# SyncE's queue walked head by head: weights loaded once per head, one output-weight buffer

## What is computed

```python
qkvz = (x @ W_qkvz).reshape(B, S, NK, 2 * DK + 2 * R * DV)     # 16 heads, R = 2
q, k, v, z = split(qkvz)
q, k, v = silu(conv4(q)), silu(conv4(k)), silu(conv4(v))
core = chunk_gated_delta_rule(l2norm(q), l2norm(k), v, g, beta)
x1 = core * silu(z)
x1 = x1 * rsqrt(mean(x1 * x1, -1) + EPS) * norm_weight
x = layernorm(x + x1.reshape(B, S, VD) @ W_out)
x = layernorm(x + ffn(x))                                       # ternary W_up, W_gate, W_down
```

## Time and profile before

| | |
|---|---|
| median of 3 executions | 4410.59 us |
| the profiled execution | 4409.74 us |
| its span, first to last instruction | 4408.0 us |
| granted TensorE clock, mean | 0.992 |
| PE busy | 4208.9 us, 95% |
| ACT busy | 3843.0 us, 87% |
| DVE busy | 3727.2 us, 85% |
| POOL busy | 2342.4 us, 53% |
| bytes moved on SP's queue | 575.59 MB, 40.6% of 16 DMA engines |

### The profile page before, as it was taken

One profiled execution on the slowest core, in us unless ns is written; L12 is line 12 of the kernel. 1 busy time (PEld: TensorE's weight loads), 2 busy tenths in 40 slices (PEclk: granted clock), 3 DMA queues, 4 the chain that ended last, 5 costly groups with the idle time before them and its releaser, 6 DMA issues. The chain is left out here.

```text
span 4408.0 us, 140088 instructions
## 1 busy us (share of the span) xinstructions
PE 4208.9 (95%) x44246; PEld 3698.7 (84%) x44246; DVE 3727.2 (85%) x6642; ACT 3843.0 (87%) x10855; POOL 2342.4 (53%) x3319
## 2 busy tenths in 40 slices
PE   3799999999999999999999999999999999999888
PEld 2688888888888888888888888888888888888745
DVE  5688888888888888888888888888888888888766
ACT  2699999999999999999999999999999999999755
POOL 3355555555555555555555555555555555555455
PEclk9999999999999999999999999999999999999999
DMA  5544444444444444444444434344444343434201
GB/s 182 180 131 146 130 145 133 142 134 141 134 140 135 140 135 140 139 136 139 136 142 132 145 130 146 129 143 132 147 128 150 125 153 122 153 123 154 72 6 34
DMA packets 450786, 584.82 MB, mean 133 GB/s; under 512 B 237472, under 2 KB 315552, under 8 KB 433184
## 3 DMA queue, kind: packets, MB, share of 16 engines
q1 hardware_dynamic: 449568, 575.59, 40.6%
q10 hardware_dynamic: 1152, 8.39, 0.5%
HBM read 533.81 MB, written 50.07 MB: 132 GB/s over the span
## 5 line engine op out<-in xcount | busy, mean ns | idle before, releaser
L1014 DVE SCALAR_TENSOR_TENSOR conv<-ps,cws,conv 128x511 f32<-128x511 f32 (+2 forms) x1536 | 1085.6, 742 | 59.8 <-ACT conv L892 39.9
L698 PE MATMUL ps<-xb,wb 128*128 128x512 f32 x3072 | 842.9, 409 | 25.7 <-DMA wb<-w_scratch 21.6
L698 PEld LDWEIGHTS ps<-xb,wb 128*128 128x128 f32 x3072 | 542.0, 190 | 127.5 <-issue 27.8
L1057 DVE CAST_PREDICATED pl<-masks,ps 128x512 f16<-128x512 uint16 x768 | 546.9, 712 | 55.3 <-PE ps L760 32.7
L953 ACT ACTIVATE t<-ps 128x512 f16<-128x512 f32 x768 | 465.9, 607 | 118.3 <-PE ps L768 107.1
L1263 POOL TENSOR_TENSOR xo<-xo,zs 128x512 f32<-128x512 f32 x128 | 163.8, 1280 | 717.0 <-DVE xo L1108 717.0
L1263 POOL TENSOR_TENSOR xo<-xo,home 128x512 f32<-128x512 f32 x128 | 162.8, 1272 | 699.4 <-DVE xo L1108 699.4
L957 ACT ACTIVATE u<-ps 128x512 f16<-128x512 f32 x768 | 473.2, 616 | 43.6 <-PE ps L773 43.6
L858 PE MATMUL ps<-wo,xt 128*128 128x256 f32 x3072 | 427.4, 289 | 33.6 <-DVE xt L1114 32.8
L712 PE MATMUL ps<-wb,xb 128*128 128x256 f32 x3072 | 428.5, 289 | 0.0
L858 PEld LDWEIGHTS ps<-wo,xt 128*128 128x128 f32 x3072 | 382.9, 190 | 47.7 <-issue 42.0
(11 more groups left out here) (188 smaller groups left out, 11701.8 us busy)
## 6 DMA issues: line engine op xcount, KB each, us to landing
xb<-x_scratch SPq DMA_DIRECT2D x128, 1024.0 KB, 5.9
wb<-w_scratch SPq DMA_DIRECT2D x128, 1024.0 KB, 5.6
decays<-rows_scratch SPq DMA_DIRECT2D x128, 512.0 KB, 3.7
wb<-w_scratch SPq DMA_DIRECT2D x128, 512.0 KB, 4.3
wo<-wout_scratch SPq DMA_DIRECT2D x128, 512.0 KB, 6.3
rk<-rk_scratch SPq DMA_DIRECT2D x128, 256.0 KB, 4.2
w_scratch<-wsplit SPq DMA_DIRECT2D x128, 192.0 KB, 3.2
wpiece<-in_Wqkvz SPq DMA_DIRECT2D x128, 96.0 KB, 2.5
```

Source lines behind the costliest of these rows:

```text
L698: last = nc.tensor.matmul(proj_bank[c][:, :], wb[:, pw, k * WCOL + c * D:k * WCOL + (c + 1) * D], xb[p][:, px, k * S:(k + 1) * S], start=( ...
L1014: nc.vector.scalar_tensor_tensor(out=conv[c][:, back:S], in0=proj_bank[c][:, 0:S - back], scalar=cws[p][:, c * TAPS + 3 - back:c * TAPS + ...
L1057: nc.vector.copy_predicated(halves(pl[l], l, 0), mask[:, None, :, :].broadcast_to([128, NU, C // (4 << l), 2 << l]), packed(p_bank, l)).th ...
```

## The change

Only SP's walk changes. It now goes through eight steps (one head) per turn of its loop, so that the stage functions know at build time which of the head's eight items, `q`, they are called for. `load_w`, `load_wz` and `load_wout` return at once unless `q` is 0. The wait on `rk_in` in `load_w` is gone; a wait on `ws_out` (the pieces of the coming head are in HBM) is added to all three. `wo` becomes a single buffer, and its load waits for the last out product of the item just before. PE's waits count heads in place of items.

```diff
-        wo = [sb(f"wo{p}", [128, 2, R, H], f32r) for p in range(2)]
+        wo = sb("wo", [128, 2, R, H], f32r)
...
+        def steps_by_head(engine, **parts):
...
+            first, last = -(-(3 - NEAR) // B), (ITS - FAR) // B
+            for s in range(-FAR, first * B):
+                step(s, s % B)
+            with engine.Fori(first, last) as j:
+                for q in range(B):
+                    step(B * j + q, q)
+            for s in range(last * B, ITS - NEAR):
+                step(s, s % B)
...
-            def load_w(a, p, _):
+            def load_w(a, q, _):
+                if q:
+                    return
+                ws_out.wait(sp, a + B - 1 - LEAD, 32)
                 proj_mm.wait(sp, a - 1, 4)
-                rk_in.wait(sp, a - 1, 16)
...
-            def load_wz(a, p, _):
+            def load_wz(a, q, _):
+                if q:
+                    return
+                ws_out.wait(sp, a + B - 1 - LEAD, 32)
                 z_mm.wait(sp, a - 1, 2)
...
-            def load_wout(b, p, _):
-                out_mm.wait(sp, b - 2, 2)
+            def load_wout(b, q, _):
+                if q:
+                    return
+                out_mm.wait(sp, b - 1, 2)
+                ws_out.wait(sp, b + B - 1 - LEAD, 32)
...
-                    pe.wait_ge(w_in.sem, w_in.at(a, 16))
+                    pe.wait_ge(w_in.sem, w_in.at(a // B, 16))
...
-                    pe.wait_ge(wz_in.sem, wz_in.at(a, 16))
+                    pe.wait_ge(wz_in.sem, wz_in.at(a // B, 16))
...
-                    pe.wait_ge(wo_in[p].sem, wo_in[p].at(b // 2, 16))
+                    pe.wait_ge(wo_in.sem, wo_in.at(b // B, 16))
```

More of the change, by code:

```diff
@@ L498, in delta_rule @@
         small_ready, cw_ready = signal("small_ready"), signal("cw_ready")
-        wo_in = [signal(f"wo_in{p}", 16) for p in range(2)]
+        wo_in = signal("wo_in", 16)
         rows_in = signal("rows_in", 16)
@@ L598, in steps, with step @@
                 step(s, s % 2)
+        def steps_by_head(engine, **parts):
+            def step(s, q):
+                for offset, stage, *n in ORDER:
+                    if stage in parts and not (isinstance(s, int) and not 0 <= s + offset < ITS):
+                        parts[stage](s + offset, (q + offset) % B, *n)
+            first, last = -(-(3 - NEAR) // B), (ITS - FAR) // B
[6 more added lines that the diff above has]
+                step(s, s % B)
         @block.sync
@@ L605, in _, with load_x @@
             sp.wait_ge(made.sem, made.at(0, MADE))
-            def load_w(a, p, _):
+            def load_w(a, q, _):
+                if q:
+                    return
+                ws_out.wait(sp, a + B - 1 - LEAD, 32)
                 proj_mm.wait(sp, a - 1, 4)
-                rk_in.wait(sp, a - 1, 16)
                 sp.dma_start(w_dst[:, :, 0:S], w_dram[ds(a // B, 1)].rearrange("a p q n -> p (a q) n")[:, :, 0:S]).then_inc(w_in.sem, 16)
-            def load_wz(a, p, _):
+            def load_wz(a, q, _):
+                if q:
+                    return
+                ws_out.wait(sp, a + B - 1 - LEAD, 32)
                 z_mm.wait(sp, a - 1, 2)
                 sp.dma_start(w_dst[:, :, S:WCOL], w_dram[ds(a // B, 1)].rearrange("a p q n -> p (a q) n")[:, :, S:WCOL]).then_inc(wz_in.sem, 16)
-            def load_x(a, p, _):
+            def load_x(a, q, _):
+                p = q % 2
                 proj_mm.wait(sp, a - 2, 4)
@@ L656, in load_norm @@
                 sp.dma_start(rk[:, :], rk_dram.broadcast_to([128, S])).then_inc(rk_in.sem, 16)
-            def load_wout(b, p, _):
-                out_mm.wait(sp, b - 2, 2)
-                sp.dma_start(wo[p][:, :, :, :].bitcast(f32), wout_dram[ds(b // B, 1)].rearrange("a p w h n -> p (a w) h n")).then_inc(wo_in[p].sem, 16)
+            def load_wout(b, q, _):
[3 more added lines that the diff above has]
+                ws_out.wait(sp, b + B - 1 - LEAD, 32)
+                sp.dma_start(wo[:, :, :, :].bitcast(f32), wout_dram[ds(b // B, 1)].rearrange("a p w h n -> p (a w) h n")).then_inc(wo_in.sem, 16)
             def ff_load(a, p, q):
@@ L675, in ff_load @@
                 sp.dma_start(FF_RAW[q].rearrange("p (k n) -> p k n", k=k), src.rearrange("(k p) n -> p k n", p=128)).then_inc(ff_in[q].sem, 16)
-            steps(sp, ff_load=ff_load, load_w=load_w, load_wz=load_wz, load_x=load_x, load_raw=load_raw, store_split=store_split, load_rows=load_rows, store_norm=store_norm, load_norm=load_norm, load_wout=load_wout)
+            steps_by_head(sp, ff_load=ff_load, load_w=load_w, load_wz=load_wz, load_x=load_x, load_raw=load_raw, store_split=store_split, load_rows=load_rows, store_norm=store_norm, load_norm=load_norm, load_wout=load_wout)
         @block.tensor
@@ L857, in out_product @@
                     for j, (h, px, pw) in enumerate(passes):
-                        last = nc.tensor.matmul(out_bank[g][:, i * H:(i + 1) * H], xt[:, px, unit(2 * g + i, h), :], wo[p][:, pw, h, :],
+                        last = nc.tensor.matmul(out_bank[g][:, i * H:(i + 1) * H], xt[:, px, unit(2 * g + i, h), :], wo[:, pw, h, :],
                                                 start=(j == 0), stop=(j == len(passes) - 1))
```

## The result

The changed kernel is slower by a quarter of a per cent: median 4421.84 us (4418.34 to 4427.78, 20 runs) against 4412.84 us (4408.23 to 4415.39, 20 runs), ratio 1.0024, 95% interval 1.0017 to 1.0031. The forecast was 4413 us in a range of 4402 to 4428, so the time lies in the range. The ratio is just past the 0.2% that counted as no change, on the side to which the prediction had given 0.17, but its interval has both sides of that line in it. The profiled execution of after took 4421.58 us with a span of 4419.8, 11.8 more than before.

What follows compares the result with a forecast made beforehand. The prediction took PE to bound the items. From a median of 4410.59 us it took -1.7 at the start and +4.5 for `rk` landing later, giving 4413 us, with an 8-in-10 range of 4402 to 4428.

Steps and rivals of the forecast that it cites:

- The frame of the prediction: Items: PE bounds them, nobody waits for the removed loads, so in the items their going is worth 0.
- The single buffer: Output weights at the head's first item: load hidden with 5.9 us to spare, cost 0; slower rival up to 94.5 us, chance 0.02.
- the `ws_out` waits and SP's long loop: On SP: stores waited for went out several steps earlier, and SP idles before the norms in every step; cost 0.
- the start: Item 1: without its z load the key norms' store comes earlier, shortening PE's wait at the gram product; -1.7 us.
- The wait on `rk_in`, taken out: Head boundaries: the 1 MB load goes out behind `rk`, which lands later; PE pays nearly whole, 15 × 0.3 = +4.5 us.
- the nearest bound: Delay of `rk` at most 0.6 us: z load, followed by 1 MB, takes 4.3 us, load of the decays 3.7.
- δ: How much later `rk` lands at each of 15 head boundaries: taken as 0.3 us, between 0 and 2.4.
- the side called slower: Over 0.2% slower, chance 0.17: `rk` late at head boundaries 0.15, single output-weight buffer 0.02.
- the prediction's own signs of being wrong: PE waiting for `wb` or `wo` after the start, DVE's boundary wait for `rk` above 0.7 us, PE's busy share above 99%.
- the far row: Last z load, with the `wo` load next behind it: took 6.0 us, 1.7 more than its median.
- The rival that fewer bytes make `rk` land sooner: Gram product: 224 MB less traffic removes 14.2 us of waits, plus 1.7 at item 1; 4395 us, chance 0.12.
- rival at 0.02: Out product: single-buffered `wo` load does not fit, PE stands up to 6.3 us at 15 heads; 4503 us, chance 0.02.

Runs made afterwards that it cites:

- the third group: Kernel before with its wait put back after the change, the change itself, and all loads by head walk, wait kept, on one chip: 4405.27, 4417.45, 4407.55 us.

## Why the forecast held its range, and which term was too small

The frame of the prediction held. The items are bound by PE, none of the removed loads was waited for, and 235 MB less moved the time by 2.3 us side by side. (The prediction's 224 MB, and the 351.6 MB to be left, count 2 MB for 2 × 1024 KB; the page has 340.68.) The single buffer is hidden, the `ws_out` waits and SP's long loop show no cost, and the start gave about the 1.7 us that the sum had for it.

The step that failed is the size of one term, in "The wait on `rk_in`, taken out": "I take 0.3, the middle of the nearest bound: 15 × 0.3 = +4.5 us". The mechanism and the place were right, and so were the 15 times and the lack of slack. At the boundaries δ was 1.1 to 1.6 us in twelve, 0.1 to 0.4 in three, and 1.2 in the mean; in the time it was 0.8 to 1.0 us per boundary. By runs of the changed kernel and of the version with the wait, the term is 12.2 to 15.3 us in place of 4.5. With it the sum is 4410.6 - 1.7 + 12.2 to 15.3 = 4421 to 4424 us, on the side called slower, which began at δ = 0.70. As a difference this is +10.5 to +13.6 us; measured were +9.0, and +10.4 in the third group, with 2.4 us of other waits gone that the sum had put at nothing. So forecast +2.8, measured +9.0: the median of before had itself risen by 2 us with more runs, and that the time lies in the range is owed to the room that the range left for δ up to 1.2. One of the prediction's own signs of being wrong came true: DVE's wait for `rk` was over 0.7 us at 13 of the 15 boundaries, 1.1 to 1.5.

What misled was, as far as can be read from the rows, the choice of the nearest one. The z load, with 1 MB of input 0.94 us behind it, takes 4.3 us, and the load of the decays 3.7, and from that δ was held to be 0.6 at most. But neither row is a load of `rk`. With nothing behind it `rk` takes 4.2 us for 256 KB, more than the decays take for 512; it was a slow transfer to begin with, and a row with less than half its time per byte was no bound for it. The last z load, with 6.0 us, 1.7 above its median, was taken for the far row and was the better guide. The rule of the Trainium skill ("DMA: Bandwidth & Descriptors", queues, rings and completion order), that an engine consumes the descriptors of one queue in ring order, pulled the same way: the prediction took δ near 0 from it. The runs agree with it in the direction, since ahead of 1 MB `rk` loses 1.4 us and behind it a 2 KB store loses 3.5. It does not follow from it that being ahead in the queue is being left alone, and here it is not.

The rival that fewer bytes make `rk` land sooner is hardly borne out: with the wait kept, the median landing of `rk` in the third group is 4.1 us with all loads and 4.0 with one in eight. The rule of the Trainium skill on double buffers ("Trainium Kernel Development and Optimization", best practices), weighed as a rival at 0.02, is not needed for this load: with one buffer, loaded for every item, the ratio was 1.0001.

What stays open: why `rk` alone is slow for its size. It reads one row of 2 KB for all 128 partitions, which had been written just before; neither the one nor the other was varied. Also open is why `rk` is hardly late at three boundaries. In the runs with part of the load behind `rk`, row length changed with the size, so bytes and row length are not told apart.

## What to carry to other kernels

Before a wait between two transfers is taken out because no data hangs on it, look at what the first of them feeds. If that chain has no slack, the wait may be what keeps the large transfer out of the small one's way, and a price for its loss is best taken from the small transfer itself, not from its neighbours. Loads that nobody waited for were worth next to nothing when they went: 235 MB of them, 2.3 us. The lowest ratio measured is that of the change with the one wait kept: 0.999 of before in one group (0.9981 to 0.9999) and 0.9992 in another (0.9983 to 1.0001), so it is at best a tenth of a per cent.

## What was not expected of the hardware

A gap in PE can cost more than its length. In the changed kernel the gram product ran at the full clock, in 1.99 us, behind all 15 boundary waits, of 0.26 to 1.57 us. With the weights ahead of the norms, behind waits of 3.2 to 4.2 us, it ran in 3.1 to 3.7 us at 14 of 15 boundaries, at a granted clock of 0.50 in the stretch shown above. The length of the wait alone does not decide: one product ran in 1.99 us behind 3.58, and at the start of the items one took 3.78 us behind 0.64.

While the broadcast of `rk` and 1 MB share the queue, the DMA engines show busy shares of five to nine tenths at 35 to 135 GB/s, and already `rk` alone shows eight or nine tenths at 41 to 181, where the 1 MB by itself runs at about 400. In this kernel the busy share of the DMA engines is no measure of what they move. And the median of one and the same kernel before differed by 5.9 us between two groups, each on its own chip (4412.9 and 4407.0), more than half of the effect under study.
